# One transformer block on one Trainium2 core: middle units taken in pairs, the products with V and the jobs each in one stretch

## The reference, cut to what matters

```
n  = gamma1 * rmsnorm(x) + beta1                   # gamma, beta: rows from t
q, k, v = split16(n @ W_q.T), split16(n @ W_k.T), split16(n @ W_v.T)      # 16 heads of 16
x1 = x + alpha1 * (softmax(0.25 * q @ k.T) @ v) @ W_o.T                    # 512 x 512 for each head
n2 = gamma2 * rmsnorm(x1) + beta2
x2 = x1 + alpha2 * ((silu(n2 @ gate.T) * (n2 @ hidden.T)) @ out_w.T + out_b)   # hidden width 1024
y  = (layernorm(x2) * w + b + tanh(t @ lin_w.T + lin_b)) * w + b
```

## Time and profile before

| what | value |
|---|---|
| median of 3 runs | 759.37 us (758.07 to 760.06) |
| the profiled execution: its own time | 758.38 us |
| its span on the core | 756.5 us |
| PE busy / DVE / ACT / POOL | 717.1 / 535.0 / 470.2 / 392.3 us |
| granted TensorE clock, mean over the span | 0.988 of full speed |

### The profile page before, as it was taken

The page is one execution under the profiler, slowest core; times in us unless marked ns, Lnnn a source line. Parts: engine busy times, 40 slices in busy tenths (PEclk is TensorE's granted clock), DMA queues, the critical chain, the costliest instruction groups (busy, mean ns, idle before and its releaser), DMA issues.

```text
span 756.5 us, 17527 instructions
## 1 busy us (share of the span) xinstructions
PE 717.1 (95%) x6660; PEld 490.3 (65%) x6660; DVE 535.0 (71%) x797; ACT 470.2 (62%) x860; POOL 392.3 (52%) x493
## 2 busy tenths in 40 slices
...
GB/s 228 168 226 243 204 168 270 125 220 137 156 58 166 191 151 137 106 200 153 141 114 140 182 144 161 61 196 151 126 155 119 186 108 3 75 105 64 49 52 29
DMA packets 63276, 107.18 MB, mean 142 GB/s; under 512 B 10480, under 2 KB 18344, under 8 KB 63192
## 3 DMA queue, kind: packets, MB, share of 16 engines
...
q0 software_dynamic: 128, 0.20, 0.1%
HBM read 57.50 MB, written 37.52 MB: 126 GB/s over the span
## 4 chain that ended last, share of the span: by engine, by line
PE 71%; DVE 10%; issue 6%; DMA 5%; ACT 3%; POOL 2%; SPq 1%; ACTq 0%; POOLq 0%; DVEq 0%
PE ps_x L1438 17%; PE ps_o L1411 12%; PE ps_j L1309 11%; PE ps_j L1451 10%; PE ps_s L1398 8%; PE ps_m L1379 6%; DVE mx L1127 3%; PE ps_o L1451 2%; DVE fx L1093 2%; ACT prob L922 2%; DVE gate_t L1167 2%; DMA d_c<-reciprocal_scratch 1%; DMA reciprocal_scratch<-d_s 1%; PE ps_m L1438 1%; PE ps_s L1438 1%
## 5 line engine op out<-in xcount | busy, mean ns | idle before, releaser
L1127 DVE TENSOR_REDUCE mx<-ps_m 128x2 f32<-128x1024 f32 x212 | 259.5, 1224 | 115.4 <-PE ps_m L1379 114.8
L922 ACT ACTIVATE prob<-ps_s 128x1024 f32<-128x1024 f32 x218 | 223.1, 1023 | 56.1 <-PE ps_s L1398 53.9
L1411 PE MATMUL ps_o<-prob,v 128*32 128x512 f32 x1024 | 137.2, 608 | 0.3 <-ACT o_raw L930 0.2
L1398 PEld LDWEIGHTS ps_s<-qs,ks 64*128 64x128 f32 x436 | 41.0, 184 | 99.4 <-issue 77.1
L1398 PE MATMUL ps_s<-qs,ks 64*128 64x512 f32 x436 | 99.8, 454 | 4.7 <-issue 3.8
L1438 PE MATMUL ps_x<-n,gh_hi 64*128 64x256 f32 x872 | 97.7, 284 | 1.7 <-DVE act_y L1174 1.6
L635 POOL TENSOR_TENSOR a_lo<-act_y,a_hi 128x256 fp32r<-128x256 f32 x100 | 73.7, 737 | 45.3 <-ACT a_hi L953 45.1
L1379 PE MATMUL ps_m<-ks,qs 64*128 64x512 f32 x424 | 88.6, 413 | 7.6 <-DVE mx L1127 3.9
L1438 PE MATMUL ps_x<-n_x,gh_hi 64*128 64x256 f32 x872 | 94.4, 276 | 0.0
L660 POOL TENSOR_TENSOR xr<-xr,sc 128x512 f32<-128x512 f32 x41 | 53.3, 1299 | 59.3 <-DVE sc L1139 40.5
L1438 PEld LDWEIGHTS ps_x<-n,gh_hi 64*128 64x128 f32 x872 | 74.2, 184 | 13.7 <-DVE act_y L1174 10.2
...
## 6 DMA issues: line engine op xcount, KB each, us to landing
...
stack_scratch<-qk_hi SPq DMA_DIRECT2D x56, 256.0 KB, 3.2
out_scratch<-o_raw SPq DMA_DIRECT2D x32, 256.0 KB, 3.7
n_x<-n SPq DMA_DIRECT2D x32, 256.0 KB, 3.7
stack_scratch<-qk_lo SPq DMA_DIRECT2D x28, 256.0 KB, 3.3
on_lo<-out_scratch SPq DMA_DIRECT2D x16, 256.0 KB
d_c<-reciprocal_scratch SPq DMA_DIRECT2D x16, 256.0 KB
```

The lines of the kernel that those rows point to most:

```text
L922: act.activation(prob[:, n % 2, 2 * h:2 * h + 2, :], score_pair(n, h)[:], ACT.Exp, scale=SCALE).then_inc(p_r, 1)
L1127: dve.tensor_reduce(mx[:, group % 2, :, h, qt], max_pair(mp)[:], AX.X, ALU.max).then_inc(mx_red, 1)
L1398: mm = pe.matmul(score_pair(n, j)[:, s, :], ks[r:r + 64, g, j, kb * P:(kb + 1) * P], qs[r:r + 64, g, j, :], start=True, stop=True)
L1411: mm = pe.matmul(ps_o[32 * i:32 * i + 32, :], v[:, g, kb, i, :], prob[:, n % 2, i, :], start=(kb == 0), stop=(kb == TT - 1), skip_group_ch ...
```

## The change

What it does, in its parts:

- **Pairs.** In units 28 to 127 `attend` is left out of odd units; an even unit ends with `attend(n - 2)` and `attend(n - 1)` in one stretch (unit 127 has one of its own). `prob` gets a third slot.
- **Jobs in other places.** The table `MIDDLE` replaces `SCHEDULE` from unit 28 on. Units with u % 4 = 1 have two jobs and the chunk: first the big one (Q or FT), then the chunk, then `MT`. Units with u % 4 = 2 have none. Q comes at u = 1 and 5 (before 3 and 11), K at 4 and 12 (before 5 and 13), FT of the second half at 13 of the same batch step (before 1 of the next). `TURN` holds the jobs of units 28 to 30.
- **Chunks** come one unit earlier (first at unit 33) and go into `ps_o`, between two groups of `attend`, not into `ps_j`. `RING` is 5.
- **Gate between the two maxima.** DVE's order is first maxima pair, gate, second pair. `tanh` writes straight into `act_y`, so it now waits for POOL's `a_low` of two steps before (`a_lo_r`), a wait that stood in DVE's gate.
- **A late job.** The `TR` of u = 15 is evacuated one unit later, behind the first maxima pair on DVE and the first exps on ACT. `FT` of unit 29 is evacuated by DVE ahead of that unit's gate.
- **Lead.** Units 24 and 25 make three maxima pairs each; from then on the lead is 7 units, so that units 121 to 127 have none (before 122 to 127). Some reads and writes of the Q and K stages move by a unit on SP.
- **Layout.** V is stored 17 columns apart, not 32; the unread output of `square` goes to `nx` or `act_y`; `gate_t` and `junk` are gone.

```diff
+MIDDLE = {0: (("TR", 1, 1),), 1: (("Q", 0, 1), ("MT", 1, 0)), 3: (("V", 0, 1),), 4: (("K", 0, 1),),
+          5: (("Q", 1, 1), ("MT", 2, 0)), 7: (("WO", 0, -1),), 8: (("WO", 1, -1),), 9: (("FT", 0, -1), ("MT", 3, 0)),
...
+TURN = {GH_AT: [("V", 1, 2)], GH_AT + 1: [("FT", 1, 0), ("MT", 0, 2)], GH_AT + 2: [("K", 1, 2)]}
...
-CHUNK_AT = GH_AT + CH + LAG
-RING = 6
+CHUNK_AT = GH_AT + CH + 1
+RING = 5
...
+def late_job(n):
+
+    if GH_AT <= n < NU and n % 2 and jobs_at(n) and jobs_at(n)[0][0] == "TR":
+        return jobs_at(n)[0]
...
-                if n > 1 and h == 0:
-                    act.wait_ge(av_done, n - 1)
-                act.activation(prob[:, n % 2, 2 * h:2 * h + 2, :], score_pair(n, h)[:], ACT.Exp, scale=SCALE).then_inc(p_r, 1)
+                if n > 2 and h == 0:
+                    act.wait_ge(av_done, n - 2)
+                act.activation(prob[:, n % 3, 2 * h:2 * h + 2, :], score_pair(n, h)[:], ACT.Exp, scale=SCALE).then_inc(p_r, 1)
...
                 act.wait_ge(gh_full, e + 1)
-                if e >= 1:
-                    act.wait_ge(y_r, e)
-                act.activation(gate_t[:], g_part(e), ACT.Tanh, scale=0.5).then_inc(t_r, 1)
+                if 2 <= e < TAIL + 2:
+                    act.wait_ge(a_lo_r, e - 1)
...
+                for m, mp in enumerate(maxima_at(n)):
+                    reduce_max(mp)
...
+                    if m == 0 and late_job(n - 1):
+                        evac(late_job(n - 1), n)
+                    if m == 0 and n == GH_AT + 1:
+                        evac(("FT", 1, 0), n)
+                    if m == 0 and 0 <= e < TAIL:
+                        gate(e)
...
             def middle_unit(n):
+                maxima = maxima_at(n)
                 scores(n, 0)
-                if n + LEAD < NU:
-                    max_scores(2 * (n + LEAD))
+                for mp in maxima[:1]:
+                    max_scores(mp)
                 gate_hidden(n - GH_AT)
                 scores(n, 1)
...
-                job(n)
-                attend(n - 1)
+                if n == GH_AT + 1:
+                    job(("FT", 1, 0))
+                for mp in maxima[1:]:
+                    max_scores(mp)
+                for what in order_at(n):
+                    if what[0] == "F":
+                        project_chunk(what[1])
+                    elif what != ("FT", 1, 0):
+                        job(what)
+                if n % 2 == 0 and n > GH_AT:
+                    attend(n - 2)
+                if n % 2 == 0 or n == NU - 1:
+                    attend(n - 1)
```

More of the change, by code:

```diff
@@ L60, in job_at, with jobs_at @@
     return (kind, i, b) if n >= 0 and 0 <= b < B and (kind, i, b) not in MOVED else None
-JOBS = PRO + [job_at(n) for n in range(LAST) if job_at(n)]
+MIDDLE = {0: (("TR", 1, 1),), 1: (("Q", 0, 1), ("MT", 1, 0)), 3: (("V", 0, 1),), 4: (("K", 0, 1),),
+          5: (("Q", 1, 1), ("MT", 2, 0)), 7: (("WO", 0, -1),), 8: (("WO", 1, -1),), 9: (("FT", 0, -1), ("MT", 3, 0)),
+          11: (("V", 1, 1),), 12: (("K", 1, 1),), 13: (("FT", 1, -1), ("MT", 0, 1)), 15: (("TR", 0, 2),)}
+TURN = {GH_AT: [("V", 1, 2)], GH_AT + 1: [("FT", 1, 0), ("MT", 0, 2)], GH_AT + 2: [("K", 1, 2)]}
+MORE = GH_AT - 4
+EARLY_MAX = 2 * (GH_AT + LEAD + 1)
+def jobs_at(n):
+    if n in TURN:
+        return TURN[n]
+    if GH_AT <= n < NU:
+        b = n // UNITS
+        return [(kind, i, b + d) for kind, i, d in MIDDLE.get(n % UNITS, ()) if 0 <= b + d < B]
+    return [job_at(n)] if job_at(n) else []
+JOB_UNIT = {job: n for n in range(LAST) for job in jobs_at(n)}
+JOBS = PRO + list(JOB_UNIT)
 JOB_NO = {job: no + 1 for no, job in enumerate(JOBS)}
@@ L76, in chunk_at, with order_at @@
     return c if n >= CHUNK_AT and (n - CHUNK_AT) % CH == 0 and c < CHUNKS else None
+def order_at(n):
+    jobs = jobs_at(n)
+    chunk = [("F", chunk_at(n))] if chunk_at(n) is not None else []
+    return [job for job in jobs if job[0] != "MT"] + chunk + [job for job in jobs if job[0] == "MT"]
+def late_job(n):
+    if GH_AT <= n < NU and n % 2 and jobs_at(n) and jobs_at(n)[0][0] == "TR":
+        return jobs_at(n)[0]
+    return None
 SC = sorted([(CHUNK_AT + CH * c, 0, ("F", c)) for c in range(CHUNKS)]
             + [(GH_AT + LAG + JC * (hf + 1), 0, ("H", hf)) for hf in range(CHUNKS * CH // JC, 2 * B)]
-            + [(n, 1, job_at(n)) for n in range(LAST) if job_at(n) and job_at(n)[0] == "WO"])
+            + [(n, 1, job) for job, n in JOB_UNIT.items() if job[0] == "WO"])
 SC_NO = {what: no + 1 for no, (_, _, what) in enumerate(SC)}
@@ L496, in unit @@
                     load_tab_b(b - 2)
-                if job_at(n - 1) and job_at(n - 1)[:2] == ("FT", 1):
-                    swap_halves(job_at(n - 1)[2], 1)
+                for job in jobs_at(n - 1):
+                    if job[:2] == ("FT", 1):
+                        swap_halves(job[2], 1)
                 if at(2, 0):
@@ L523, in unit @@
                     max_rows(b, 2)
+                if at(6, 1) and n >= GH_AT:
+                    stack_read(b + 1, 0)
+                if at(7, 1) and n >= GH_AT:
+                    stack_write(b + 1, 2)
                 if at(8, 1):
@@ L750, in unit @@
                     n_low(b + 1, 1)
-                if job_at(n - 1) and job_at(n - 1)[:2] == ("FT", 1) and n < NU:
-                    n2_low(job_at(n - 1)[2], 1)
+                for job in jobs_at(n - 1) if n < NU else []:
+                    if job[:2] == ("FT", 1):
+                        n2_low(job[2], 1)
                 if at(5 if b == 1 else 4, -1):
@@ L830, in square1 @@
             def square1(b, t):
+                if t == 0 and b > 1:
+                    act.wait_ge(n_lo_r, 2 * b)
                 if b == 0 and t == 0:
@@ L1028, in unit @@
                     square2(b - 1, 0, 1)
-                if job_at(n) and GH_AT <= n < NU:
-                    evac(job_at(n), n)
+                for job in jobs_at(n) if GH_AT <= n < NU else []:
+                    if job != late_job(n):
+                        evac(job, n)
                 if u == 0 and 0 < n <= NU:
@@ L1256, in unit @@
                     scale(("H", 2 * (b - 2) + 1))
-                if 0 <= e < TAIL:
+                if 0 <= e < TAIL and not maxima_at(n):
                     gate(e)
@@ L1262, in unit @@
                     statistics(b - 3, 1)
-                if chunk_at(n) is not None:
-                    scale(("F", chunk_at(n)))
-                if job_at(n) and n < NU:
-                    evac(job_at(n), n)
+                for what in order_at(n) if n < NU else []:
+                    if what[0] == "F":
+                        scale(what)
+                    elif what not in (late_job(n), ("FT", 1, 0)):
+                        evac(what, n)
                 if at(3 if b == 1 else 2, -1):
```

130 lines of the change are left out of this document (64 added, 66 removed).

## The result

The changed kernel takes 761.32 us (759.32 to 764.27, 11 runs), the kernel before, on the same chip, 758.07 us (757.05 to 760.06, 11 runs): a ratio of 1.0039, interval 1.0026 to 1.0052. It is 0.4% slower, where 754.8 was forecast. The profiled execution has 764.27 us of its own time (span 762.5), the longest of its kernel's 11, so its trace shows more than a median execution loses. Lost clock is no peculiarity of it: the mean granted clock of the 11 executions is 0.979 to 0.986, the median 0.982, as in the profiled one. The kernel before has 0.984 to 0.991 in its runs beside the experiments, median 0.988.

A forecast was written before the change was run, and what follows sets the result against it. PE bounds the kernel, waiting only 3.0 us a batch. Units 48 to 95 -4.3, 32 to 47 -0.6, 96 to 127 -3.2, 28 to 31 +2.8, 24 and 25 +0.7: -4.6 from 759.37, so 754.8 us; range 747 to 761.

The forecast's parts named there:

- Fewer changes of kind: PE from unit 28 on: 321 changes between product kinds become 248, saving drains and fills, 9.7 us together.
- The rival by the rule of the Trainium skill on MT: MT on PE counts as its own tiling mode, 24 more changes: 2.4 us less gain, 757.2; chance 3%.
- The loop of the gate between the maxima: DVE's gate delays the second reduction, so a unit with maxima takes at least 4.32 us, whatever PE holds.
- my sign of being wrong: The prediction would be wrong if u = 3 took 4.15 us, its PE work without a wait.
- the loop and the exps set 3.53 for 111 and 115: Units 111 to 126, odd units empty of jobs: stretch of 74.9 us; units 96 to 127 159.9, 3.2 less.
- Units 28 to 31: FT evacuated ahead of unit 29's gate makes it 7.1 long; the four units take 21.8 us, a loss of 2.8.
- The staging buffer: At u = 5 Q(1) follows K(0) through one staging buffer; the forecast's batch sum held no wait for it.
- the rival that had one: MT at u = 5 waits if K(0)'s write lands late; at 6 us, 2.3 us a batch, 768; chance 12%.
- At nothing: V's layout, `RING` 5, third `prob` slot, squares' output and tanh's wait for `a_low` were forecast to cost nothing.
- Lead and units 24 and 25: Units 24 and 25 hold one more reduction each: 0.7 us more, which comes back in unit 121.
- The dear loop: The gate loop is dearer or hits more units, 0.8 us more a batch, nothing left: 759.4; chance 20%.
- The cheap loop: Waits of u = 15 and 29 overlap others and the 9.7 us come in whole: 749.7; chance 22%.

The follow-up runs named there:

- experiment 10: Changed kernel with Q(0)'s staging write issued at u = 2 and K(0)'s ahead of `o_write` on SP: 757.69 us, ratio 0.9987 to the kernel before.
- experiment 3: Changed kernel plus 16 identity products on PE in units 29 and 30, which nothing reads: 758.34 us, ratio 0.9991 to the kernel before.
- experiment 2: Changed kernel with DVE's gate put back behind both maxima pairs: 754.78 us, ratio 0.9951 to the kernel before.
- 4: Changed kernel with K(0)'s staging write issued ahead of `o_write` on SP: 760.37 us, ratio 1.0028 to the kernel before.
- 5: Changed kernel with FT of unit 29 evacuated last on DVE, not ahead of the gate: 758.19 us, ratio 0.9996 to the kernel before.
- 9: Changed kernel with Q(0)'s staging write issued at u = 2, not u = 3, on SP: 759.28 us, ratio 1.0013 to the kernel before.
- 11: Changed kernel with the gate behind both maxima pairs and both staging writes (Q(0), K(0)) early: 752.79 us, ratio 0.9921 to the kernel before.
- 12: Changed kernel with gate behind both maxima, both staging writes early and 16 idle products in units 29 and 30: 752.71 us, ratio 0.9928 to the kernel before.

## Why the prediction was wrong, step by step

**Fewer changes of kind: right.** u = 2 at 4.41 for 4.42, a stretch of products with V 1.85 for 1.87, MT without a drain. In experiment 10, which has every part of the change and only the two writes moved, units 32 to 95 take 344.5 us for the 343.6 forecast, and units 96 to 127 take 160.4 for 159.9. The rival by the rule of the Trainium skill on MT (3%) did not come: the same rows show no drain between chunk and MT.

**The loop of the gate between the maxima: right in length, wrong in what it does.** From first maxima to first maxima it is 4.34 to 4.41 us behind u = 3, 7, 11 and 15, for the 4.32 forecast, and the waits of the batches came to no more than I had summed. They lie at the starts of u = 0, 4, 8 and 12, as expected. So my sign of being wrong, a u = 3 of 4.15, was badly chosen: u = 3 takes 4.2 and u = 7 4.16, although the wait is there. That it could also halve the clock I had not priced. Forecast for units 96 to 127: -3.2; measured 0.0. Units 112 and 116 hold 3.0 of that, 6.73 and 6.74 for the 5.22 that both show in experiments 3 and 10. In experiment 2 the loop is taken out and they are 5.04. This is one of the failed steps: "the loop and the exps set 3.53 for 111 and 115 [...] Sum 159.9" held the waits and left out the clock behind them. No run fills the waits at these two units with idle products, so the price is read from the same two units with and without the fall, not from an edit that touches the clock alone.

The fall at these units is no fixed price. Among the six profiled kernels with the gate between the maxima and the pairs whole (after, 3, 4, 5, 9, 10) unit 112 fell once and unit 116 four times out of six. The five with the gate last had none. PE's waits are the same in all twelve cases, 1.01 to 1.03 and 0.54 to 0.55; in experiment 10 both units pass with the clock at 1.00. What decides between the two stays open.

**Units 28 to 31: the second failed step.** Forecast +2.8, measured +5.75. Units 29 and 30 were to take 13.1 together, and took 15.84. The waits were right: unit 30's maxima were to come 7.47 after the start of unit 29 and came after 7.58. (Unit 30's scores go ahead of that wait, so that it lies in unit 30 and unit 29 is 5.87 long, not near 7.) What failed is the 6.0 for unit 30, which took its products at the full clock. From its maxima to its end that is 5.66; it took 8.26 in after and 5.78 in experiment 3, where the clock stays at 1.00. So 2.5 us are half the clock behind "DVE evacuates FT ahead of unit 29's gate", which makes PE wait 2.05 and then 1.21. The price scatters: with the same two waits unit 30 takes 9.8 to 10.1 in after, 4 and 9 and 8.83 in experiment 10. Taking away the early evacuation (5) gives 3.1 us back, though the clock still falls.

**The staging buffer: the third failed step.** u = 5 was forecast with no wait for it, and the rival that had one (12%) sized it at 2.3 us in each batch. It came in two batches of five, as 1.1 and 1.4 us (u = 5 at 8.42 and 8.68 for 7.30), and scatters: from 7.29 (experiment 3) to 9.68 (experiment 2) in batch 4 of the other kernels that keep Q(0)'s write in its place. Its path is mostly not the rival's. The rival had MT wait for Q(1)'s copy; MT waits in batch 4 alone, 0.65. The rest is the second scores, 1.08 in batch 2 and 0.52 in batch 4: K(0)'s own copy waits 3.28 and 2.73 for Q(0)'s write, and the exps stand behind it on ACT. I had counted SP's issues around K(0)'s write and none around Q(0)'s, which stands behind the reciprocal's landing. The landing of K(0)'s write was as I had it: 3.3 us from the last issue in batches 3 and 5, 3.5 and 4.3 in 2 and 4, where I had 3.5. That of Q(0)'s, for which I had no term, takes 4.8 to 6.1. Experiments 9 and 10 show the chain: two writes moved on SP are 3.6 us of the median. Of these 2.5 are u = 5 by the profile of after; the rest isn't located.

**At nothing: nearly right.** tanh waits for `a_low` once from unit 28 on, 0.7 us in unit 125, and never in units 48 to 95. No wait for the third `prob` slot or the ring shows. Lead and units 24 and 25: the start of unit 28 lies within what the same code scatters by.

**The rivals.** The dear loop (759.4) was near by the number and not by its reason: 0.8 us more of loop waits in each batch did not come. The cheap loop (749.7) came in no run; nearest are 11 and 12 (752.8 and 752.7), which take the loop out.

**The forecast as a whole** was off by 6.5 us in the median. As a difference to the kernel before it was off by 7.8, -4.6 forecast and +3.2 measured, since the median of before was 759.37 in three runs and is 758.07 in eleven. Three causes are of a like size in the profiled execution, which is 10.5 above its forecast: half a clock behind the waits of units 29 and 30 (2.5), the same at units 112 and 116 (3.0), and the place of two DMAs in SP's queue (2.5). The others are all under 1 us. How the three divide the 6.5 us of the median was not measured. None was in the sum of PE's own work and its waits for DVE, which in experiment 10 came out within 1 us in each stretch from unit 32 on.
